# Attention scores of two heads on row halves of TensorE, with the mask added there, in a macaron block on one core

## The reference

```python
x = x + 0.5 * ffn(_layernorm(x)); x = x + attn(_layernorm(x)); x = x + 0.5 * ffn(_layernorm(x))
# attn: 16 heads of 16, rotary embedding on q and k
att = jnp.einsum('bhqd,bhkd->bhqk', q, k) / math.sqrt(hd)
att = jax.nn.softmax(att + mask, axis=-1)        # mask: -inf where key > query
out = jnp.einsum('bhqk,bhkd->bhqd', att, v)      # then (B, T, D) @ Wo.T
# ffn: silu((x @ gate_w.T) * gate_s) * ((x @ up_w.T) * up_s) @ down_w.T * down_s, 704 inner
```

## Time and profile before

| | us |
|---|---|
| median of three runs (lowest, highest) | 1101.89 (1100.88, 1103.45) |
| profiled execution, own time | 1104.99 |
| its span | 1103.3 |
| busy: PE, DVE, ACT, POOL | 971.9, 835.4, 533.3, 397.8 |
| mean granted TensorE clock, share of full speed | 0.933 |

### The profile page before, as it was taken

One profiled execution on the slowest core, in us unless ns is written; L12 is line 12 of the kernel. 1 busy time (PEld: TensorE's weight loads), 2 busy tenths in 40 slices (PEclk: granted clock), 3 DMA queues, 4 the chain that ended last, 5 costly groups with the idle time before them and its releaser, 6 DMA issues.

```text
span 1103.3 us, 16962 instructions
## 1 busy us (share of the span) xinstructions
PE 971.9 (88%) x5624; PEld 680.6 (62%) x5624; DVE 835.4 (76%) x2188; ACT 533.3 (48%) x1152; POOL 397.8 (36%) x650
## 2 busy tenths in 40 slices
PE   6798997898898898998989889898898898899895
PEld 4677776655565565655655556565564554787785
DVE  5798888788786686877868778686686675878984
ACT  3142222445565564645656555565665567223230
POOL 5376666522241222323313224130221211445652
PEclk9899899989998988988989999898998899999998
DMA  8000000221111111211112111111111120000001
GB/s 293 1 1 1 1 1 1 60 51 40 29 47 33 38 36 26 55 29 35 31 31 54 34 31 32 29 48 34 38 41 36 43 83 2 1 29 30 30 30 39
DMA packets 36283, 41.43 MB, mean 38 GB/s; under 512 B 10704, under 2 KB 23248, under 8 KB 36192
## 3 DMA queue, kind: packets, MB, share of 16 engines
q1 hardware_dynamic: 32528, 36.81, 12.3%
q0 software_dynamic: 3520, 3.42, 1.4%
q10 hardware_dynamic: 144, 0.07, 0.0%
HBM read 10.30 MB, written 4.19 MB: 13 GB/s over the span
## 4 chain that ended last, share of the span: by engine, by line
PE 75%; DVE 12%; issue 9%; ACT 2%; POOL 0%; DMA 0%; DVEq 0%; ACTq 0%
PE psum L774 16%; PE psum L756 13%; PE psum L787 13%; PE psum L692 13%; PE psum L648 9%; PE psum L815 5%; DVE XN_f L991 3%; PE psum L659 2%; DVE NP L1103 2%; PE psum L795 1%; DVE HF_f L1022 1%; ACT NMT L909 1%; PE psum L745 1%; DVE T_f L965 1%; DVE XNa L1070 1%
## 5 line engine op out<-in xcount | busy, mean ns | idle before, releaser
L920 ACT ACTIVATE PT<-psum 128x512 f32<-128x512 f32 (+3 forms) x768 | 344.4, 496 | 260.7 <-PE psum L774 254.4
L756 PE MATMUL psum<-K,Q 96*128 96x512 f32 (+2 forms) x768 | 271.6, 388 | 64.3 <-issue 60.2
L774 PE MATMUL psum<-Q,K 100*128 100x512 f32 (+2 forms) x768 | 296.3, 408 | 1.3 <-ACT NMT L909 0.5
L1107 DVE CUSTOM_DVE_ANT_0 psum<-psum,STRIP 128x384 f32<-128x384 f32 (+3 forms) x512 | 236.3, 518 | 31.9 <-PE psum L756 31.6
L774 PEld LDWEIGHTS psum<-Q,K 100*128 100x128 f32 x768 | 151.8, 201 | 142.6 <-ACT PT L920 61.4
L1103 DVE TENSOR_REDUCE NP<-psum 128x1 f32<-128x512 f32 x256 | 165.2, 683 | 93.0 <-PE psum L756 92.5
L756 PEld LDWEIGHTS psum<-K,Q 96*128 96x128 f32 x768 | 152.6, 203 | 96.3 <-issue 68.1
L787 PE MATMUL psum<-PT,V 128*32 128x512 f32 (+3 forms) x1536 | 167.6, 509 | 2.0 <-ACT OS L929 1.5
L1250 POOL TENSOR_SCALAR_AFFINE_SELECT PT<-PT 128x512 f32<-128x512 f32 x128 | 81.3, 636 | 234.7 <-ACT PT L920 234.6
L692 PE MATMUL psum<-XH_f,WGH_f 128*128 128x512 f32 x352 | 146.9, 417 | 8.2 <-issue 8.2
L692 PE MATMUL psum<-XL_f,WGH_f 128*128 128x512 f32 x352 | 144.0, 409 | 0.3 <-DVE XL_f L997 0.3
(11 more groups left out here) (95 smaller groups left out, 1214.6 us busy)
## 6 DMA issues: line engine op xcount, KB each, us to landing
Q<-GH SPq DMA_DIRECT2D x128, 64.0 KB, 2.0
K<-GH SPq DMA_DIRECT2D x158, 32.0 KB, 1.9
Q<-GL SPq DMA_DIRECT2D x64, 64.0 KB, 2.0
out<-X SPq DMA_DIRECT2D x16, 256.0 KB, 2.2
K<-GL SPq DMA_DIRECT2D x124, 32.0 KB, 1.9
X<-x SPq DMA_DIRECT2D x7, 512.0 KB, 8.7
K<-GH POOLq DMA_DIRECT2D x98, 32.0 KB, 2.0
RG_f<-wgu SPq DMA_DIRECT2D x6, 384.0 KB, 5.0
```

Source lines behind the costliest of these rows:

```text
L756: nc.tensor.matmul(bank(*step)[:, 0:nn], q[0:96, p, t * P:(t + 1) * P], k[0:96, p, hh, ch * 512:ch * 512 + nn], start=True, stop=True).the ...
L774: nc.tensor.matmul(bank(*step)[:, base:512], k[0:100, p, hh, j * P:(j + 1) * P], q[0:100, p, 512 * c2 + base:512 * c2 + 512], start=True, ...
L920: sc.activation(PT[n % 3][:, h, 0:512 - skip], bank(*step)[:, skip:512], ACT.Exp, scale=0.25).then_inc(sem("act_exp"), 1)
L1107: v.tensor_tensor_reduce(out=bank(*step)[:, 0:n], in0=bank(*step)[:, 0:n], in1=STRIP[:, 512 - n:512], scale=-1.0, scalar=BIG, op0=ALU.add, ...
```

## The change

Scores and heads come in pairs p of two heads. Head hh of a pair lies on rows 64 hh to 64 hh + 47 of `Q` and `K` (high, high, low against high, low, high, 16 rows each), with its shift in two rows below. The two matmuls of a pair use the two halves of the array's rows and write two neighbouring banks. K loses its index hh and its zeros. For diagonal scores PE adds the mask with four more matmuls from a bf16 table `MASK` (an identity in its first two planes, the masks in the others), two for each 64 queries. DVE takes plain maxima over both banks, ACT exp over both banks. Q and K have three buffers; one `move` a group sends 24 pieces of 16 rows and 1024 columns, all on the SP queue, and each `rows` sends four pieces. Pairs take banks (0, 1), (2, 3) or (4, 5); a single product takes the one of banks 0 to 6 that was taken longest ago. The timetable moves with it. In the feed-forward stages the bank numbers and the places of some tiles in memory change, and POOL writes `MASK` once before it splits the projection weights.

```diff
 def score_steps(gr, c2):
-    return [(512 if ch < c2 else (t % 4 + 1) * P, ("score", gr, t, ch, h))
-            for ch in range(c2 + 1) for t in range(4 * c2, 4 * c2 + 4) for h in range(4)]
+    return [(512 if ch < c2 else (t % 4 + 1) * P, ("score", gr, t, ch, p))
+            for ch in range(c2 + 1) for t in range(4 * c2, 4 * c2 + 4) for p in range(2)]
...
     if gr + 2 < 4 * NG:
-        plan += [(0.6, ("stack", gr + 2, 0)), (0.74, ("move", gr + 2, 0)), (0.9, ("stack", gr + 2, 1))]
-        late[gr + 1].append((0.07, ("move", gr + 2, 1)))
+        plan += [(0.16, ("stack", gr + 2, 0)), (0.2, ("stack", gr + 2, 1)), (0.24, ("move", gr + 2))]
     side = []
     if b + 1 < B:
-        for pr in ((0,) if b else (), (1, 2), (3,), ())[g]:
+        for pr in ((0, 1) if b else (1, 2), (2, 3) if b else (3,), (), ())[g]:
             side += qkv_steps(b + 1, pr)
     if b:
-        for pr in ((0,), (), (1,), (2, 3))[g]:
+        for pr in ((), (), (0, 1), (2, 3))[g]:
             side += oproj_steps(b - 1, pr)
...
-    beside[7, 2] = [("keys_zero", 0, 0), ("stack", 0, 0), ("stack", 0, 1)]
-    beside[7, 3] = [("move", 0, 0), ("keys_zero", 0, 1)]
-    beside[7, 4] = [("move", 0, 1)]
+    beside[7, 2] = [("stack", 0, 0), ("stack", 0, 1)]
+    beside[7, 3] = [("keys_ones", 0), ("move", 0)]
...
-    out += [s for _, s in tiles1[:4]] + [("rows", 0, 0)] + [s for _, s in tiles1[4:10]]
-    out += [("stack", 1, 0), ("move", 1, 0), ("stack", 1, 1)]
+    out += [s for _, s in tiles1[:2]] + [("rows", 0, 0), ("stack", 1, 0), ("stack", 1, 1), ("move", 1)]
+    out += [s for _, s in tiles1[2:5]]
...
-    small, many = [0, 7], [0, 1, 2, 3, 4, 5, 6]
-    rings = {"xpose": [5, 6], "gu": [1, 2, 3, 4], "down": [0, 7], "small": small, "many": many}
+    rings = {"gu": [0, 1, 2, 3], "xpose": [4, 5], "down": [6, 7], "small": [6, 7]}
+    choice = {1: [(b,) for b in (6, 0, 1, 2, 3, 4, 5)], 2: [(0, 1), (2, 3), (4, 5)]}
...
+        if ring == "any":
+            put(product, *min(choice[n], key=lambda bs: max(taken[b] for b in bs)))
+            return
...
-        def wait_qk_free(eng, gr, half):
-            if gr >= 2:
-                wait_heads(eng, gr - 2, half)
-            elif gr == 1:
+        def wait_qk_free(eng, gr):
+            if gr >= 3:
+                wait_heads(eng, gr - 3)
+            elif gr:
                 wait_first_ffn(eng)
...
-                    nc.tensor.matmul(bank(*step)[:, 0:nn], q[0:96, p, t * P:(t + 1) * P],
-                                     k[0:96, p, hh, ch * 512:ch * 512 + nn], start=True, stop=True).then_inc(sem("pe_s"), 1)
+                    for hh in range(2):
+                        rows = slice(64 * hh, 64 * hh + 48)
+                        ins = nc.tensor.matmul(dst[:, hh, 0:nn], q[rows, p, t * P:(t + 1) * P],
+                                               k[rows, p, ch * 512:ch * 512 + nn], start=True, stop=not diagonal)
+                    if diagonal:
+                        for half in range(2):
+                            for hh in range(2):
+                                rows = slice(64 * hh, 64 * hh + 64)
+                                ins = nc.tensor.matmul(dst[:, hh, n - P + 64 * half:n], MASK[rows, half, :],
+                                                       MASK[rows, 2 + half, 64 * half:P], start=False, stop=half == 1)
+                    ins.then_inc(sem("pe_s"), 1)
...
-                    nc.tensor.matmul(bank(*step)[:, base:512], k[0:100, p, hh, j * P:(j + 1) * P],
-                                     q[0:100, p, 512 * c2 + base:512 * c2 + 512], start=True, stop=True).then_inc(
-                        sem("pe_st"), 1)
+                    for hh in range(2):
+                        rows = slice(64 * hh, 64 * hh + 50)
+                        ins = nc.tensor.matmul(dst[:, hh, base:512], k[rows, p, j * P:(j + 1) * P],
+                                               q[rows, p, 512 * c2 + base:512 * c2 + 512], start=True, stop=True)
+                    ins.then_inc(sem("pe_st"), 1)
...
-                    sc.activation(PT[n % 3][:, h, 0:512 - skip], bank(*step)[:, skip:512], ACT.Exp, scale=0.25).then_inc(
-                        sem("act_exp"), 1)
+                    sc.activation(PT[n % 3][:, 2 * p:2 * p + 2, 0:512 - skip], bank_pair(*step)[:, :, skip:512], ACT.Exp,
+                                  scale=0.25).then_inc(sem("act_exp"), 1)
...
-                        v.tensor_tensor_reduce(out=bank(*step)[:, 0:n], in0=bank(*step)[:, 0:n], in1=STRIP[:, 512 - n:512],
-                                               scale=-1.0, scalar=BIG, op0=ALU.add, op1=ALU.min, accum_out=acc).then_inc(
-                            sem("dve_max"), 1)
+                    v.tensor_reduce(out=NP[gr % 2][:, 0 if diagonal else 1, t, 2 * p:2 * p + 2],
+                                    in_=bank_pair(*step)[:, :, 0:n], axis=AX, op=ALU.max, negate=True).then_inc(
+                        sem("dve_max"), 1)
...
+                    sp.wait_ge(*upto("act_gh", "stack", gr, 1))
+                    sp.wait_ge(*upto("dve_gl", "stack", gr, 1))
+                    wait_qk_free(sp, gr)
+                    for dst, src in pieces(gr):
+                        sy.dma_start(dst, src).then_inc(sem("dma_qk"), 16)
```

More of the change, by code:

```diff
@@ L140, in group_steps @@
         for n, u in enumerate(us):
-            for h in range(4):
-                out.append(("head", *u, h))
-                if h == 3:
+            for p in range(2):
+                out.append(("head", *u, p))
+                if p == 1:
                     pend.append(u)
-                now = (sum(room[:n]) + room[n] * (h + 1) / 4) / sum(room)
+                now = (sum(room[:n]) + room[n] * (p + 1) / 2) / sum(room)
                 while at < len(plan) and plan[at][0] < now:
@@ L209, in psum_banks @@
         if kind == "scores_begin":
-            side = "many"
+            side = "any"
         elif kind == "scores_end":
@@ L221, in psum_banks @@
         elif kind == "down_all":
-            for pr, tt, b in ((0, 0, 5), (0, 1, 6), (1, 0, 0), (1, 1, 7)):
+            for pr, tt, b in ((0, 0, 4), (0, 1, 5), (1, 0, 6), (1, 1, 7)):
                 put(("down_all", s[1], pr, tt), b)
         elif kind == "flag_all":
-            put(s, 0)
-        elif kind in ("a_turn", "o_turn", "qk", "val", "stack", "score", "rows", "head", "divide", "proj"):
+            put(s, 6)
+        elif kind in ("a_turn", "o_turn", "qk", "val", "stack", "rows", "divide", "proj"):
             take(side, s)
+        elif kind in ("score", "head"):
+            take(side, s, 2)
         elif kind == "weigh" and s[3] == 0:
@@ L286, in counts @@
             add("act_o", s[1:3])
-        elif kind == "head" and s[4] == 3 and s[3] >= 4 * s[2]:
+        elif kind == "head" and s[4] == 1 and s[3] >= 4 * s[2]:
             add("pool_mask", s[1:4])
-        elif kind == "move":
-            cut = key_cut(s[1])
-            add(f"dma_k{s[2]}", s, 16 * cut)
-            add(f"dma_kp{s[2]}", s, 16 * (12 - cut))
         elif kind == "shift":
@@ new lines, in wait_bank @@
+            for old in bank_before[product]:
+                kind = old[0]
+                if kind == "xpose":
+                    eng.wait_ge(*upto("dve_xl", *old))
+                elif kind == "gate" and old[3] < 5:
+                    eng.wait_ge(*upto("act_silu", "gu", *old[1:]))
+                elif kind in ("gate", "up"):
+                    eng.wait_ge(*upto("dve_h", "gu", *old[1:]))
+                elif kind == "down":
+                    eng.wait_ge(*upto("dve_t2", *old[1:]))
+                elif kind == "down_all":
+                    eng.wait_ge(*upto("dve_t2", old[1], 7, old[2]))
+                elif kind == "flag_all":
+                    eng.wait_ge(sem("dve_flag"), 8)
+                elif kind in ("a_turn", "o_turn"):
+                    eng.wait_ge(*upto("dve_ll", *old))
+                elif kind == "qk":
+                    eng.wait_ge(*upto("dve_rope", *old))
+                elif kind == "val":
+                    eng.wait_ge(*upto("act_v", *old))
+                elif kind == "stack":
+                    eng.wait_ge(*upto("dve_gl", *old))
+                elif kind == "score":
+                    eng.wait_ge(*upto("dve_max", *old))
+                elif kind == "rows":
+                    eng.wait_ge(*upto("act_nt", *old))
+                elif kind == "head":
+                    eng.wait_ge(*upto("act_exp", *old))
+                elif kind == "weigh":
+                    eng.wait_ge(*upto("act_o", *old[1:]))
+                elif kind == "divide":
+                    eng.wait_ge(*upto("dve_on", *old))
+                else:
+                    assert kind == "proj", old
+                    eng.wait_ge(*upto("dve_xp", *old))
@@ L902, in scalar_program @@
                     act.wait_ge(*upto("pe_zT", *step))
-                    wait_g_free(act, gr, half)
-                    sc.activation(GH2[half][:, :], bank(*step), ACT.Copy).then_inc(sem("act_gh"), 1)
```

(19 more changed lines are left out.)

252 lines of the change are left out of this document (95 added, 157 removed).

## The result

Four runs of the changed kernel took 1051.17 to 1076.55 us, median 1057.52, against 1102.67 before: the ratio is 0.956, with a 95% interval of 0.948 to 0.964. So it is some 48 us faster, where 102 were forecast. The profiled execution took 1052.96 us.

The account below looks back on a forecast made before the run. The attention stretch was taken as PE-bound with a hole in each group; -144 + 48 + 38 - 60 - 24 + 30 + 10 = -102 from 1104.99, and 3 off, gave 1000 us, range 925 to 1075.

Parts of the forecast that it names:

- step 4: Q and K transfers before scores: three buffers and whole-group moves end the 16 stalls, -60 us, and the lower clock after, -24.
- rival B: Attention stretch: three bank pairs and DVE set the pace, -40, 1062 us; sign DVE and ACT 25% or more; chance 0.20.
- step 7: Waits of the attention stretch: three bank pairs not a bound, short waits grow from 57 to 87 us, +30 (0 to +95).
- step 1: Scores and heads on PE: 736 pairs at 0.24 us each, 0.18 at full overlap, -144 us (0 to -186).
- step 3: PE between scores or heads and other products: 192 places leave and re-enter an array shape, 0.20 a change, half taken, +38 us.
- Step 2: Diagonal scores on PE: four more mask matmuls a step at 0.20 us, some 240 steps, +48 us (26 to 106).
- Step 5: Maxima on DVE: one reduction over two banks, 1.13 us for 1024 columns, DVE's 512 us become about 465.
- Step 8: Start of the attention stretch: all 24 transfers must land before scores, +6 us, and ACT waits in group 0, +4.

Follow-up runs that it names:

- e1: The changed kernel with pairs only on banks (0, 1) and (2, 3), single products on 4, 5 and 6: 1281.5 us, ratio 1.164.
- e15: e11 with scores and heads on 112 and 114 rows of a constant tile instead of their halves of Q and K: 1016.6 us, ratio 0.924.
- e16: e4 with scores and heads on 112 and 114 rows of a constant tile instead of their halves of Q and K: 1071.0 us, ratio 0.975.
- e9: The changed kernel with every head a product of its own, on one of seven banks in turn, still on row halves: 1062.9 us, ratio 0.966.
- e2: The changed kernel with each score pair's two matmuls issued twice: 1076.8 us, ratio 0.978.
- e4: The changed kernel with the 1024 mask matmuls left out: 1056.6 us, ratio 0.960.
- e11: e9 with the mask back on DVE and no mask matmuls on PE: 1039.7 us, mean of two runs, scattering up to 1067.0.
- e6: The kernel before, with SP sending only 3 of the 15 transfers of a half from group 2 on: 1010.7 us, ratio 0.916.
- e8: The changed kernel with projections back to one batch pair a group: 1081.7 us, ratio 0.979.
- e10: e9 with one projection pair of the next batch a group and earlier transfers than e8: 1097 and 1110 us.

## Why the prediction was wrong

The direction was right, and so was step 4 with its mechanism; the size of the whole was not: -48 us instead of -102. The time lay near rival B (1062), and B's sign is there too: of the chain from first head to last PE has 56% and DVE and ACT together 31%, where the forecast had 85% and 10 to 15%, and B 25% or more.

**The step that failed is 7.** It let the short waits grow from 57 to 87 us, beside 501 of PE. Measured in the chain from first to last head, everything that isn't PE has 281 us, and PE 367. The working computed 390 us at full use of the three pairs of banks and called it "not a bound". The measure that mattered was not their use but what each engine does while its next pair is not yet filled: a bank is free only when the reader of both is done, PE refills two at a time, and it walks one order, so it may be in a weighing or a projection. e1 shows how steep this is: +229 with two pairs. And e15 against e16 shows it with the same work on PE: single banks leave 113 us of the chain to everything else, pairs of banks 216.

Single banks alone don't bring the forecast either. In e9 everything else has 87 us, as step 7 had it, but PE has 567 where the forecast had 501. Part of that is e9's own: some 295 products have lost their overlap, by estimate up to 53 us at step 1's mean of 0.18. The rest says that the sum of PE's steps was too small as well. By the steps below it is an estimated 22 to 51 us in the changed kernel: 22 less for the mask, 44 to 73 more for the shapes.

One reading under step 3 was also wrong. The head of 0.43 in the earlier trace rows stands before a stall, so its time runs to its end. Where another step follows at once, a 512-column head behind a weighing takes 0.34 to the next start, here in the kernel before. The median of 60 such places is 0.34 too, against 0.24 behind a score or another head, so leaving the weighing costs 0.10 and not 0.20.

```profile
505.99 0.50 PE L774 MATMUL psum<-Q,K 100*128 100x512 f32 x1
506.33 0.52 PE L756 MATMUL psum<-K,Q 96*128 96x256 f32 x3
```

The steps one by one:

- Step 1, pairs: a pair of 512 columns takes 0.24 us, as taken; that is also the median in e2, where the second of two score pairs waits for nothing. But its -144 was booked as time of the span. e2 puts a third of the added work there, and e16 against e4 gives all of step 1 less the changes of shape: -14.
- Step 2, mask: 0.10 a step, not 0.20. It is worth nothing at the end in the changed kernel (e4), and some 23 us with single banks (e9 against e11).
- Step 3, shapes: the measured cost sits in three places, before the other product, in it and behind it. I took medians from one start to the next in e15 and e9, which have the same plan on full rows and on row halves. Before four turns 0.24 became 0.33, the turns went from 0.36 to 0.59, and the product behind them takes 0.02 more: 0.34 in all. Before six projection matmuls 0.24 became 0.42, they went from 1.38 to 1.59, and the product behind them from 0.23 to 0.34: 0.49 in all. Over 192 places that is an estimated 65 to 94 us of PE, around the upper end of 77 where I had taken half. Each of the 192 weighings is also entered 0.09 later, 17 us. The Trainium skill's rule that a change of tiling mode drains TensorE (TensorEngine Tiling (Array Packing), Key Properties) agrees with these numbers.
- Step 4, buffers and stalls: forecast -84, measured -93 (e6) and -83 for the whole new plan with single banks and full rows (e15 against its before, start included). Right.
- Step 5, DVE: 1.14 for 1024 columns, 1.13 forecast, right. Step 8, the beginning: +10 forecast, +11.1 measured.

Two ways lead from the kernel before to the changed one. By e15, e16 and e4 it is -83 (plan and buffers), +54 (pairs of banks), -14 (row halves), -4 (mask). By e15, e11 and e9 it is -83, +23 (row halves), +23 (mask on PE), -10 (pairs of banks). Both end at -47 by construction, so the sums prove nothing; what they show is that the scores' new form as a whole costs 36 us, and that no share of it belongs to one part alone. What also stays open is whether the bunched projections cost: e8 and e10 were both slower by other things.

## What to carry to other kernels

In a stage whose engines are coupled through few buffers there may be no single engine to relieve: take a resource away (a buffer) or double a piece of work, and read from the time what it is worth, before counting saved engine time as saved span. When two readers' steps are merged over two banks, count what the writer can have filled ahead, in steps of the reader, not the total use. And try the cheapest cure of a named wait first: here the wait before scores was SP's issue time of 0.62 us a transfer, and one number that moves four transfers to another queue gave more than the whole change.

## What the runs showed of the hardware

With row halves TensorE was mostly granted a lower clock at nearly the same busy time, but not always. Here are e11 and then e15, three stretches each (columns as in the earlier trace rows); PE is busy 146 to 149 of 150 us in each:

```profile
300.00:450.00 150.00, 146.02 (x905) 72.73 (x904) 124.14 (x382) 98.28 (x240) 35.50 (x83) 0.91 0.27 44
450.00:600.00 150.00, 148.00 (x956) 78.87 (x952) 129.28 (x399) 101.07 (x240) 34.80 (x82) 0.99 0.27 44
600.00:750.00 150.00, 147.72 (x946) 77.15 (x942) 123.92 (x382) 98.46 (x241) 34.46 (x81) 0.94 0.25 41
```

```profile
300.00:450.00 150.00, 147.47 (x933) 90.22 (x935) 128.05 (x406) 102.51 (x249) 35.81 (x83) 1.00 0.27 44
450.00:600.00 150.00, 149.19 (x947) 95.06 (x948) 128.95 (x387) 98.94 (x234) 38.06 (x94) 1.00 0.26 44
600.00:750.00 150.00, 149.07 (x967) 94.06 (x966) 126.61 (x396) 103.09 (x247) 31.68 (x70) 1.00 0.26 44
```

With row halves the granted clock is 0.91 to 0.99 of full speed, so the engine spends part of the time at 1.2 instead of 2.4 GHz; on full rows it is 1.00. The kernels with pairs of banks, one stretch each of e4 (row halves), e16 (full rows) and e2 (row halves, each score pair twice):

```profile
450.00:600.00 150.00, 134.55 (x902) 65.81 (x901) 109.46 (x171) 87.87 (x142) 34.75 (x82) 0.92 0.23 39
...
450.00:600.00 150.00, 141.53 (x897) 86.63 (x891) 108.28 (x168) 85.67 (x138) 35.15 (x82) 1.00 0.21 35
...
450.00:600.00 150.00, 141.47 (x1299) 79.19 (x1295) 107.11 (x165) 85.63 (x137) 34.55 (x81) 1.00 0.20 34
```

So a lower clock doesn't simply follow from the row halves: e2 has them and is granted 1.00. What sets e2 apart from e4 is not shown. Busy time goes by the records' modelled ends, and counts two overlapping halves once. e15 and e16 read constant operands, which could matter too; against that stands e6, whose 96 and 100 rows hold changing operands and which is granted 1.00 with PE busy 148.5 of 150 us. In the kernel before, on full rows too, the clock was 0.53 after a stall.
